# The keys of the second and third chunk multiplied right behind the scores, with ScalarE copying them in four parts

## The reference, cut to what matters

```
q = relu(q) + EPS;  k = relu(k) + EPS
k_cumsum = cumsum(k, axis=2)
context = cumsum(einsum('bhnd,bhne->bhnde', k, v), axis=2)
D_inv = 1.0 / einsum('bhnd,bhnd->bhn', k_cumsum, q)
attn = einsum('bhnd,bhnde,bhn->bhne', q, context, D_inv)
x = x + attn @ Wo + bo                      # of layernorm(x)
h = silu(fp4(x') @ fp4(w_gate).T) * (fp4(x') @ fp4(w_up).T)
x = x + fp4(h) @ fp4(w_down).T
```

## Time and profile before

| | us |
|---|---|
| runs, median of 3 | 1511.81 (1509.83 to 1518.97) |
| the profiled execution | 1515.2 |
| its span, first to last instruction | 1513.5 |
| PE busy | 1462.2 (97%) |
| DVE busy | 1148.1 (76%) |
| ACT busy | 640.0 (42%) |
| POOL busy | 725.0 (48%) |
| mean granted PE clock | 0.995 |

### The profile page before, as it was taken

One profiled execution on the slowest core, in us unless ns is written; L12 is line 12 of the kernel. 1 busy time (PEld: TensorE's weight loads), 2 busy tenths in 40 slices (PEclk: granted clock), 3 DMA queues, 4 the chain that ended last, 5 costly groups with the idle time before them and its releaser, 6 DMA issues.

```text
span 1513.5 us, 54703 instructions
## 1 busy us (share of the span) xinstructions
PE 1462.2 (97%) x23324; PEld 1369.8 (91%) x23324; DVE 1148.1 (76%) x2363; ACT 640.0 (42%) x1124; POOL 725.0 (48%) x822
## 2 busy tenths in 40 slices
PE   8889999999999999999999999999999999999998
PEld 7878899899999889998999999999999999999888
DVE  7786678677777777778777777777778777777767
ACT  5433444344453334533444433444444443453433
POOL 4313554544554435554445544545454544555443
PEclk9999999999999999999999999999999999999999
DMA  4101244354443444443453543544444354443310
GB/s 169 30 6 43 75 137 137 94 167 114 142 141 107 119 129 139 128 128 110 131 153 112 143 133 94 156 126 141 128 133 138 99 166 117 136 141 113 118 50 15
DMA packets 188880, 176.24 MB, mean 116 GB/s; under 512 B 16224, under 2 KB 174944, under 8 KB 188640
## 3 DMA queue, kind: packets, MB, share of 16 engines
q1 hardware_dynamic: 188640, 172.75, 39.2%
HBM read 89.59 MB, written 83.10 MB: 114 GB/s over the span
## 4 chain that ended last, share of the span: by engine, by line
PE 59%; DMA 9%; issue 8%; DVE 8%; POOL 5%; SPq 4%; ACT 2%; POOLq 0%; DVEq 0%; ACTq 0%
PE bank L650 46%; DMA hq_away<-hq_blocks 3%; DMA attn_away<-probs 3%; PE bank L783 3%; PE bank L734 2%; PE bank L817 2%; DMA attn<-attn_away 2%; PE bank L851 2%; POOL attnT_lo L1578 2%; SPq L585 2%; DVE attn L1948 1%; SPq L568 1%; DVE hq_blocks L2025 1%; POOL hqT_lo L1590 1%; PE bank L929 1%
## 5 line engine op out<-in xcount | busy, mean ns | idle before, releaser
L650 PE MATMUL bank<-xT_hi,wqk_hi 128*128 128x256 f32 x1024 | 212.2, 288 | 7.4 <-ACT qkT L1171 3.8
L1578 POOL TENSOR_TENSOR attnT_lo<-attn,attnT_hi 128x1024 fp32r<-128x1024 f32 x58 | 154.3, 2660 | 121.8 <-ACT attnT_hi L1258 121.8
L650 PE MATMUL bank<-xT_lo,wqk_hi 128*128 128x256 f32 x1024 | 204.4, 281 | 0.0
L650 PE MATMUL bank<-xT_hi,wqk_lo 128*128 128x256 f32 x1024 | 204.3, 281 | 0.0
L1171 ACT ACTIVATE qkT<-bank 128x512 f32<-128x512 f32 x256 | 147.1, 589 | 79.7 <-PE bank L650 79.4
L1638 POOL TENSOR_SCALAR qkT<-qkT 128x512 f32<-128x512 f32 x256 | 158.0, 631 | 41.0 <-ACT qkT L1171 39.9
L650 PEld LDWEIGHTS bank<-xT_hi,wqk_hi 128*128 128x128 f32 x1024 | 158.2, 189 | 11.9 <-issue 8.7
L650 PEld LDWEIGHTS bank<-xT_hi,wqk_lo 128*128 128x128 f32 x1024 | 157.3, 189 | 0.0
L650 PEld LDWEIGHTS bank<-xT_lo,wqk_hi 128*128 128x128 f32 x1024 | 157.2, 189 | 0.0
L1617 POOL TENSOR_TENSOR xq<-x_scaled,x_scale 128x256 f32<-128x256 f32 x64 | 49.6, 775 | 220.5 <-DVE x_scaled L1804 214.6
L1308 ACT ACTIVATE silu<-bank 128x352 f32<-128x352 f32 x128 | 58.4, 457 | 210.6 <-PE bank L650 210.4
(11 more groups left out here) (220 smaller groups left out, 3810.2 us busy)
## 6 DMA issues: line engine op xcount, KB each, us to landing
attn<-attn_away SPq DMA_DIRECT2D x232, 128.0 KB, 3.1
hq_away<-hq_blocks SPq DMA_DIRECT2D x58, 384.0 KB, 3.0
hq<-hq_away SPq DMA_DIRECT2D x232, 96.0 KB, 2.3
keys_away<-key_stage SPq DMA_DIRECT2D x41, 512.0 KB, 2.9
key_stage<-keys_away SPq DMA_DIRECT2D x164, 128.0 KB, 3.2
attn_away<-probs SPq DMA_DIRECT2D x58, 256.0 KB, 2.9
attn_away<-probs SPq DMA_DIRECT2D x116, 128.0 KB, 3.1
x_in<-in_L_attn_x SPq DMA_DIRECT2D x32, 256.0 KB, 2.9
```

Source lines behind the costliest of these rows:

```text
L650: at = pe.matmul(dst, lhs_at(kt), rhs_at(kt), start=first and kt == 0, stop=last and kt == k_tiles - 1)
L1578: pool.tensor_tensor(by_raw_attn(attnT_lo), attn_raw, by_raw_attn(attnT_hi).bitcast(F32), ALU.subtract).then_inc(attnT_ready, 2)
```

## The change

The early keys of the second and third chunk (c of 1 and 2, among `SENT_KEYS`: 27 chunks) leave `attend` and are called right behind `scores`, ahead of the transposes of `xq` and of `project_v`. For these chunks ACT's one copy becomes four: two of the early rows (64 rows, 512 columns each), which wait for the DMA and the previous early keys alone, and two of the late rows, which wait for `kv_done` and stand behind `high_sent_attn`. A new semaphore `late_k_ready` counts the late parts; PE's `late_keys` of the next step and DVE's `block_keys` wait for it. Three entries of the bank table are dealt anew. The bank of `xq` in the third chunk is now 1, which the late keys of that step hold before it and the probabilities by values take after it.

```diff
--- before.py
+++ after.py
@@ -194,7 +194,7 @@
         scores_done, probs_ready = sem("scores_done"), sem("probs_ready")
         kv_early_done, state_mid_ready = sem("kv_early_done"), sem("state_mid_ready")
         late_keys_done = sem("late_keys_done")
-        k_turned, k_ready = sem("k_turned"), sem("k_ready")
+        k_turned, k_ready, late_k_ready = sem("k_turned"), sem("k_ready"), sem("late_k_ready")
         crossed_done = sem("crossed_done")
         key_blocks_ready, keys_sent, keys_back = sem("key_blocks_ready"), sem("keys_sent"), sem("keys_back")
         av_done, den_ready, attn_ready = sem("av_done"), sem("den_ready"), sem("attn_ready")
@@ -290,14 +290,14 @@
         }
         steady = {
             "x": [(0,), (), (7,), ()],
-            "scores": [(5, 3), (3, 6), (6, 2), (2, 5, 7, 3)],
+            "scores": [(5, 3), (6, 7), (6, 2), (2, 5, 7, 3)],
             "k": [(1, 6), (4, 7), (0, 1), ()],
-            "xq": [(4,), (4,), (5,), (0,)],
+            "xq": [(4,), (4,), (1,), (0,)],
             "v": [(2, 7), (5, 0), (7, 3), (6, 0)],
             "kv": [(0, 1), (3, 4), (4, 5), ()],
             "av": [(3, 4, 5, 6), (6, 7, 1, 2), (6, 7, 0, 1), (1, 2, 4, 5)],
             "gate_up": [(7, 4, 5, 0), (7, 3, 5, 2), (5, 3, 6, 4), (4, 5, 3, 7)],
-            "late_kv": [(), (1, 2), (3, 4), (0, 1)],
+            "late_kv": [(), (1, 2), (0, 1), (0, 1)],
             "qk": [(), (5, 0, 5, 6, 4, 6, 0, 1), (), (7, 3, 7, 1, 6, 1, 2, 4)],
             "wo": [(3,), (2,), (6,), (2,)],
             "down": [(1,), (5,), (2,), (7,)],
@@ -473,6 +473,9 @@
 
         def sent_keys(n):
             return len([g for g in SENT_KEYS if g < n])
+
+        def parted_keys(n):
+            return len([g for g in SENT_KEYS if g < n and g % CHUNKS])
 
         def turned_keys(n):
 
@@ -789,20 +792,21 @@
 
                 kv = [banks.take(pe, ("late_kv", place(g), n), b, state_ready, lambda b: (CHUNKS - 1) * b + c)
                       for n in range(2)]
+                if g - 1 in SENT_KEYS and c > 1:
+                    pe.wait_ge(late_k_ready, 2 * parted_keys(g))
                 keys_by_values(c - 1, kv, True).then_inc(kv_done, 1)
 
+            def early_keys(b, c, g, u):
+                pe.wait_ge(v_ready, 4 * (u + 1))
+                pe.wait_ge(k_ready, 2 * ((CHUNKS - 1) * b + c + 1))
+                kv = [banks.take(pe, ("kv", place(g), n), b, state_mid_ready, lambda b: (CHUNKS - 1) * b + c + 1)
+                      for n in range(2)]
+                keys_by_values(c, kv, False).then_inc(kv_early_done, 1)
+
             def attend(b, c, g, u, between):
-                pe.wait_ge(v_ready, 4 * (u + 1))
                 v = v1[c // 2]
-
-                def early_keys():
-                    pe.wait_ge(k_ready, 2 * ((CHUNKS - 1) * b + c + 1))
-                    kv = [banks.take(pe, ("kv", place(g), n), b, state_mid_ready, lambda b: (CHUNKS - 1) * b + c + 1)
-                          for n in range(2)]
-                    keys_by_values(c, kv, False).then_inc(kv_early_done, 1)
-
-
-                early_keys()
+                if c == 0 or g not in SENT_KEYS:
+                    early_keys(b, c, g, u)
 
                 to = [[banks.take(pe, ("av", place(g), 2 * half + odd), b, attn_ready,
                                   lambda b, half=half: 2 * (CHUNKS * b + c) + half + 1) for odd in range(2)]
@@ -1024,6 +1028,8 @@
                         turn_k(b, c, g)
                 else:
                     last_scores(b, c, g, u)
+                if c and g in SENT_KEYS:
+                    early_keys(b, c, g, u)
                 turn_weights(jobs_at(g, "scores"))
                 if gated and not turned_late:
                     turn_xq(b, c, g - 2)
@@ -1240,9 +1246,30 @@
                 act.activation(k_tok[:].rearrange("p (n a e) -> p n a e", n=PAIRS, a=GROUPS), staged_keys, ACT.Copy
                                ).then_inc(k_ready, 2)
 
+            def part_of_keys(late):
+                whole = k_tok[:].rearrange("p (n a e) -> p n a e", n=PAIRS, a=GROUPS)
+                for half in range(2):
+                    rows = key_rows(half * HALF_PAIRS, late)
+                    pairs = slice(half * HALF_PAIRS, (half + 1) * HALF_PAIRS)
+                    yield whole[rows, pairs], staged_keys[rows, pairs]
+
+            def early_staged_keys(b, c):
+                act.wait_ge(keys_back, 16 * GROUPS * (sent_keys(CHUNKS * b + c) + 1))
+                act.wait_ge(kv_early_done, (CHUNKS - 1) * b + c)
+                for to, got in part_of_keys(False):
+                    act.activation(to, got, ACT.Copy).then_inc(k_ready, 1)
+
+            def late_staged_keys(b, c):
+                act.wait_ge(kv_done, (CHUNKS - 1) * b + c)
+                for to, got in part_of_keys(True):
+                    act.activation(to, got, ACT.Copy).then_inc(late_k_ready, 1)
+
             def keys_by_tokens(b, c):
                 if CHUNKS * b + c in SENT_KEYS:
-                    staged_keys_to_tokens(b, c)
+                    if c:
+                        early_staged_keys(b, c)
+                    else:
+                        staged_keys_to_tokens(b, c)
                 else:
                     for n in range(2):
                         keys_to_tokens(b, c, n)
@@ -1391,6 +1418,8 @@
                     keys_by_tokens(b, c)
                 if g - 1 in SENT_ATTN:
                     high_sent_attn(g - 1)
+                if c and g in SENT_KEYS:
+                    late_staged_keys(b, c)
                 if g > WARM:
                     square_h(g - 3)
                 if g not in SENT_KEYS:
@@ -1414,6 +1443,8 @@
                     square_x(g - 2)
                 evacuate_v(c, u + 1, 1, 1 - c // 2, part=(1,))
                 high_sent_attn(g - 1)
+                if g in SENT_KEYS:
+                    late_staged_keys(b, c)
                 if is_late(g - 2) and c == 3:
                     square_x(g - 2)
                 square_h(g - 3)
@@ -1932,7 +1963,10 @@
                 dve.wait_ge(qk_ready, PAIRS * u + PAIRS // 2)
                 if n != SENT_KEYS[0]:
                     before = SENT_KEYS[sent_keys(n) - 1]
-                    dve.wait_ge(k_ready, 2 * ((CHUNKS - 1) * (before // CHUNKS) + before % CHUNKS + 1))
+                    if before % CHUNKS:
+                        dve.wait_ge(late_k_ready, 2 * parted_keys(n))
+                    else:
+                        dve.wait_ge(k_ready, 2 * ((CHUNKS - 1) * (before // CHUNKS) + before % CHUNKS + 1))
                 dve.transpose(key_blocks, qkT[:, PAIRS:2 * PAIRS, t * P:(t + 1) * P].rearrange(
                     "p n (j c) -> p n j c", c=GROUP)).then_inc(key_blocks_ready, 1)
```

## The result

| | before | after |
|---|---|---|
| median of the runs, us | 1511.64 (7 runs, 1507.32 to 1518.97) | 1526.11 (7 runs, 1523.42 to 1534.13) |
| profiled execution, us | 1515.2 | 1523.4 |
| its span | 1513.5 | 1521.6 |
| PE's listed waits from 225 to 1440 us, all rows added up | 23.0, 24 times | 28.5, 39 times |

The account below looks back on a forecast made before the run. PE, busy 97% of the span, was taken as the bound. Terms of -11.3, +1.5, +9.8 and -2 gave -2.0 us on the profiled 1515.2, or 1513.2; less 3.4 to the median, the forecast was 1509.8 us, range 1500 to 1520.

Parts of the forecast that it names:

- Gaps of instruction blocks: PE's stops in runs of small matmuls, second and third chunks: shorter runs (160 to 128) remove 80%, -11.3 us.
- The new run of 128 in front of the projection: PE's 128 small matmuls now ahead of the value projection: three instruction blocks come late, 0.5 us each, +1.5 us.
- The second chunk's wait: PE waits 0.7 us for the early keys' copies in fourteen second chunks, where nothing waited before: +9.8 us.
- rival A: Second chunk: copies of 64 rows cost half, the wait is 0.2 us, 7 us more are gained: 1502.8 us, chance 0.12.
- The third chunk's early parts: Third chunk: the early copies end at 818.1 and PE asks at 818.54, so no wait.
- The third chunk's late parts: Third chunk: two late copies push `xqT_lo` back 1.07 us, but PE, already 0.7 us late, finds it ready: 0 us.
- rival B: ScalarE and DVE slip too; PE waits 0.3 to 0.5 us for `xqT_lo` in 13 third chunks: 1517.0 us, chance 0.20.
- What the delay gives back: PE comes 0.7 us later per sequence, which saves half of 4.5 us of its other waits: -2 us.
- C: PE's issue gaps don't depend on how dense the matmuls stand; they remain and only move: 1519.6 us, chance 0.10.
- The sum: All terms for the whole kernel: -2.0 us on the profiled 1515.2, or 1513.2 us.

## Why the prediction was wrong, step by step

- **Gaps of instruction blocks: right in size, half right in cause.** Forecast: -11.3 us. The listed gaps fell by 10.0 us, from 12 to 5, which with 0.2 each is -11.4. That the sizes agree is partly luck, for the length of the run was not all of it: with one bank dealt anew and the run of 160 untouched, the four gaps of third chunks went too. The prediction also misread its rows: the four of the earlier trace rows are 20.8 us in 21 waits, not 18.8 in 18, and of its ten gaps four (5.4 us) lie in third chunks and six (6.6 us) in second ones, not seven and three. The gap at 1423.93, which the earlier trace rows calls the last of third chunks, is in the second chunk g = 61. The total of 12.1 stands.
- **The new run of 128 in front of the projection: right, but hidden.** Forecast: +1.5 us for three blocks. In the change no wait at the early keys of a second chunk is longer than the copy makes it. Where that wait is away, such gaps are there: three, 1.95 us listed, with both copies moved, and four, 2.4 us, with the early parts alone.
- **The second chunk's wait: right in mechanism, too small.** The term was "Fourteen second chunks (g = 9 to 61): +9.8 us" at 0.7 each. It is 0.95 to 0.97 each, +13.3. Two parts take 1.27, not 1.07. The row I went by, two copies of 128x512 in 1.07, reads a PSUM bank; the early parts read SBUF. The prediction's sentence under rival A, that ScalarE's rows have one price per column count whatever they read, is not so in its own trace. ACT's rows of the kernel before that read SBUF would have given the price, 626 ns for 512 columns and 1058 for 1024:

```profile
L1258 ACT ACTIVATE attnT_hi<-attn 128x1024 fp32r<-128x1024 f32 x58 | 61.4, 1058 | 41.9 <-DMA attn<-attn_away 29.7 <-issue 12.0
...
L1204 ACT ACTIVATE hq_blocks<-silu 128x512 bf16<-128x512 f32 x2 | 1.3, 626 | 0.0
```

  The changed kernel shows 624 and 631 for 64 rows of 512 columns:

```profile
L1265 ACT ACTIVATE k_tok<-key_stage 64x512 f32<-64x512 f32 x54 | 34.1, 631 | 1.3
L1260 ACT ACTIVATE k_tok<-key_stage 64x512 f32<-64x512 f32 x54 | 33.7, 624 | 9.2 <-DMA key_stage<-keys_away 8.6
```

  Besides, two copies from a bank overlap by 0.11 us (1.07 for twice 0.59), and these don't. The Trainium skill, "VectorE: DVE Perf Modes", section "The TRN2 errata", says that ScalarE pays a fixed cost more per instruction when it reads SBUF; from the two entries of its table I estimate 43 ns for that. The rows agree in kind, and with 626 ns out of SBUF against 589 out of a bank (`qkT`) they measure 37.
- **The third chunk's early parts: right in ten of 13.** In three PE waits for them (0.46, 0.56 and 1.53 us), and there ACT itself had waited 1.5 to 2.6 us for the DMA.
- **The third chunk's late parts: this is the step that failed.** "If it keeps its time, PE finds `xqT_lo` ready, so I take 0; the other case is rival B." It was not 0 but 7.1 us listed in 8 waits, 8.7 with 0.2 each. Three things were missed. The late parts take 1.29 of ACT's time in a chain that begins when the attention comes back and has no slack. Probabilities take not bank 1 alone but also bank 7, which the value copies read, and these stand last in that chain; the prediction's term names only `xqT_lo`. And the delay that PE brings from the second chunk covered 3.5 us at most: without it, in the kernel with third chunks alone, the wait is 12.2 us, with it 8.7. That the late parts were the cause is shown by moving them: with them behind the value copies the waits for ACT went from 7.1 to 0.2 us and the time by 10 us.
- **What the delay gives back: about that size in the trace, but not shown to come from the delay.** Forecast -2. The waits in first chunks fell from 3.5 us in 5 to 1.7 in 4, 2.0 with 0.2 each. But with both copies moved, and so without the delay, they are 1.7 in 3 as well.
- **The rivals.** A (half a price for half the rows) fell with 624 ns for 64 rows. C (the gaps stay) fell with 10 us of gaps less. What B said came true, in 8 third chunks instead of 13 and with 0.2 to 1.4 us instead of 0.3 to 0.5, but its reason, that ACT and DVE slip with PE in the second chunk, is not needed: the waits stood in 12 third chunks of the kernel whose second chunks are those of before.
- **The sum.** 1513.2 by the prediction's terms, +8.7 for the third chunk, +3.5 for the second and -1.5 for the run whose gaps were hidden are 1523.9; the profiled execution took 1523.4. The listed waits agree: from 23.0 us in 24 to 28.5 in 39, with 0.2 each that is +8.5, and the profiled executions stand 8.2 apart. The rest of the miss is the step from the profiled execution to the median: the prediction took off 3.4 us, and the change's own profiled execution lies 2.7 below its median instead. The granted clock of the two, 0.995 and 0.998, is of the size to account for this.

## What to carry to other kernels

When a multiplication is moved ahead of the work that covered its operand's copy, price the copy by rows that read the same memory, not only the same shape. When a chain of copies starts at a DMA's return, whoever waits for its last member can pay for every instruction put into it, so list all banks that the waiting step takes and where each is freed. And try the bank alone first: here one entry of the table brought some 7 us, and no kernel with the moved work was faster than that.

## What was not expected of the hardware

- 64 rows cost ACT as much as 128: 0.63 us for 512 columns out of SBUF.
- Blocks of 256 instructions stopped PE for 0.2 to 1.9 us listed in a 97% busy kernel, at places that moved when 64 instructions were added ahead. A comparison of two orders on PE can hold some microseconds of this; here the 64 idle instructions moved the gaps and happened to leave the time as it was (0.9997).
- A gap can be due to a wait that is over before it: in four third chunks the block was asked for only after the wait for `xqT_lo`, and PE stopped 2.3 to 2.6 us after the end of that wait.
